# Three pairs of accumulator banks, coefficients by VectorE, ungated row gathers, and sparser breaks in the front's gathers

## The reference, cut to what matters

```python
z = jnp.einsum('ni,hoi->nho', h, Wfc)                       # 3750 x 8 x 64
e = jax.nn.leaky_relu(s_src[src] + s_dst[dst], negative_slope=NEG_SLOPE)
m = jax.ops.segment_max(e, dst, num_segments=N)
ex = jnp.exp(e - m[dst])
denom = jax.ops.segment_sum(ex, dst, num_segments=N)
alpha = ex / denom[dst]
msg = alpha[:, :, None] * z[src]
out = jax.ops.segment_sum(msg, dst, num_segments=N)
```

## Time and profile before

| | us |
|---|---|
| median of 3 runs | 4323.76 |
| lowest and highest run | 4310.84, 4329.1 |
| the profiled execution, device time | 4364.62 |
| its span, first to last instruction | 4362.9 |
| aggregation of layer 0, POOL's first gather to the end | 578.7 to about 1440 |
| aggregation of layer 1 | 2886.9 to about 3765 |

### The profile page before, as it was taken

How to read it: one execution, slowest core, us unless ns; L and a number is a source line. 1 busy time by engine, 2 the same in 40 slices (tenths; PEclk the granted TensorE clock), 3 DMA queues, 4 the chain that set the end, 5 groups by cost and what they waited for, 6 DMA issues and landing times. The chain is left out here.

```text
span 4362.9 us, 56022 instructions
## 1 busy us (share of the span) xinstructions
PE 3068.3 (70%) x12306; PEld 2004.9 (46%) x12307; DVE 2384.3 (55%) x4094; ACT 932.0 (21%) x2416; POOL 1617.7 (37%) x1595
## 2 busy tenths in 40 slices
PE   6957547777777784299995966637777777555990
PEld 2423235555555453255542433325555555454760
DVE  5756655555565786723324123565555555786444
ACT  2100012222222561011111200012222222341210
POOL 0565035555555000144431455135555555101215
PEclk9978768888898885599997987858888888757995
DMA  4315235555555112055555253124545555215336
GB/s 143 91 57 95 76 111 146 145 149 145 147 146 150 47 73 87 18 127 148 148 127 136 76 127 71 59 87 141 146 141 144 143 145 144 73 58 176 120 121 222
DMA packets 330652, 513.30 MB, mean 118 GB/s; under 512 B 172484, under 2 KB 177860, under 8 KB 329744
## 3 DMA queue, kind: packets, MB, share of 16 engines
q0 software_dynamic: 113824, 311.79, 26.8%
q1 hardware_dynamic: 92720, 194.54, 12.7%
q10 hardware_dynamic: 123840, 3.94, 1.6%
HBM read 423.20 MB, written 86.92 MB: 117 GB/s over the span
## 5 line engine op out<-in xcount | busy, mean ns | idle before, releaser
L898 POOL DMA_INDIRECT aggregate_zg<-z_rows,src_groups x940 | 890.6, 947 | 1061.0 <-SPq L906 480.6
L965 PE MATMUL bank<-aggregate_msg,aggregate_onehot 128*128 128x260 f32 x2816 | 818.5, 443 | 108.6 <-DVE aggregate_msg L932 77.7
L965 PEld LDWEIGHTS bank<-aggregate_msg,aggregate_onehot 128*128 128x128 f32 x2816 | 580.5, 217 | 215.7 <-issue 124.0
L932 DVE TENSOR_TENSOR aggregate_msg<-aggregate_zg,bank 128x1024 f32<-128x1024 f32 x528 | 639.8, 1212 | 11.2 <-SPq L911 5.3
L862 ACT COPY acc<-bank x530 | 313.9, 592 | 1221.0 <-PE bank L952 632.7
L927 DVE TENSOR_SCALAR aggregate_onehot<-bank,step_base,dst_groups 128x128 f32<-128x128 f32 x704 | 256.8, 406 | 503.3 <-PE bank L952 171.5
L369 POOL DMA_INDIRECT front_d<-src_scores,src_chunks x320 | 319.5, 998 | 347.2 <-DMA front_d<-src_scores,src_chunks 182.9
L952 PE MATMUL bank<-zero_bf 128*128 128x2 bf16 x1060 | 122.2, 171 | 301.3 <-ACT acc L862 217.0
L952 PEld LDWEIGHTS bank<-zero_bf 128*128 128x128 bf16 x1060 | 111.0, 105 | 438.8 <-issue 375.3
L965 PE MATMUL bank<-aggregate_msg,s_src 128*128 128x260 f32 x704 | 236.6, 466 | 59.2 <-DVE aggregate_msg L932 49.1
L1584 POOL DMA_INDIRECT exp_xg<-hn_rows,exp_gather_tok x64 | 71.9, 1124 | 537.0 <-DVE exp_gather_tok L1646 415.9
(11 more groups left out here) (378 smaller groups left out, 4204.7 us busy)
## 6 DMA issues: line engine op xcount, KB each, us to landing
exp_w<-in_L_ffn_w SPq DMA_DIRECT2D x32, 1024.0 KB
slot_out<-exp_y SPq DMA_DIRECT2D x66, 256.0 KB
z_rows<-front_z SPq DMA_DIRECT2D x60, 256.0 KB
hn_rows<-fin_xn SPq DMA_DIRECT2D x20, 768.0 KB, 3.4
aggregate_zg<-z_rows,src_groups POOLq DMA_INDIRECT x940
front_early<-src_key SPq DMA_DIRECT2D x16, 640.0 KB
front_early<-src_tile SPq DMA_DIRECT2D x16, 640.0 KB
front_edge<-src_key SPq DMA_DIRECT2D x16, 640.0 KB
```

The costliest lines, as they stand in the source:

```text
L898: pool.indirect_dma_start(zg[:, r, j, :], None, k.z_rows[:, :], bass.IndirectOffsetOnAxis(k.src_groups[:, n:n + 1], 0)).then_inc(gathered[ ...
L932: v.tensor_tensor(msg[:, m, :, 0:HD].rearrange("p u (h d) -> p u h d", d=DH), z, bcast_last(scale[n % COEF].rearrange("p (u h) -> p u h", ...
L965: nc.tensor.matmul(k.banks[:, bank(t, half), 0:HW].rearrange("p a n -> p (a n)"), lanes_of(n % OS, j), msg[:, m, j * 2 + half, :], start=F ...
```

## The change

In the aggregation there are three pairs of accumulator banks, used in turn. DVE builds, for each step, one packed register value in `step_tile`: the tile in the upper bits, and the first banks of the present, the next and the previous pair in three fields below. PE's opening of step n waits for `evict(n)`, where it waited for `evict(n+1)`. The lane numbers are read from SBUF (`k.iota`) and not from PSUM. The coefficients are copied to banks 6 and 7 by DVE, 16 groups at a time (15 copies in a layer), and ACT's copy to `scale` and its wait for `msg_ready` are gone; PE, and no longer DVE, waits for `prepared`. POOL's wait for the gather three before is gone. In the front, POOL waits after every eighth gather or scatter.

```diff
@@ front
-                            if c % 4 == 2:
+                            if c % 8 == 4:
                                 pool.wait_ge(gathered[i * J + j], 16 * c)
...
-                    if n % 4 == 2:
+                    if n % 8 == 4:
                         pool.wait_ge(scattered, 16 * n)
...
+                    tile, third, last = steps_i[0:1, 1, :], steps_i[0:1, 0, :], steps_f[0:1, :]
+                    packed = k.step_tile[:, LATE:]
+                    v.tensor_scalar(packed, tile, 512.0, 272.0, ALU.mult, ALU.add)
+                    chain(v.tensor_scalar(third, tile, 43.0, None, ALU.mult))
+                    chain(v.tensor_single_scalar(third, third, 7, ALU.logical_shift_right))
+                    chain(v.scalar_tensor_tensor(third, third, -3.0, tile, ALU.mult, ALU.add))
+                    v.tensor_scalar(last, third, 2.0, None, ALU.is_equal)
+                    chain(v.scalar_tensor_tensor(packed, third, -238.0, packed, ALU.mult, ALU.add))
+                    chain(v.scalar_tensor_tensor(packed, last, 336.0, packed, ALU.mult, ALU.add))
...
@@ aggregate
-        lanes = k.ps[4][:, 0:P]
-        scale = [k.ps[5 + u][:, 0:J * H] for u in range(COEF)]
+        lanes = k.iota[:, :]
+        scales = k.banks[:, 6:8, :].rearrange("p b n -> p (b n)")
+        scales_ready = sem("scales_ready")
...
                     act.wait_ge(evicted, n + 1)
-                    t = act.value_load(k.step_tile[0:1, bass.ds(n, 1)], min_val=0, max_val=NT - 1)
+                    x = act.value_load(k.step_tile[0:1, n:n + 1], min_val=0, max_val=(NT - 1) * 512 + 272)
                     act.wait_ge(summed, n + (HEAD - 1))
-                    nc.scalar.copy(k.acc_all[:, bass.ds(t * 2, 2), :], k.banks[:, bass.ds(((t + 1) & 1) * 2, 2), 0:HW]).then_inc(evicted, 1)
+                    nc.scalar.copy(k.acc_all[:, bass.ds((x >> 9) * 2, 2), :], k.banks[:, bass.ds((x >> 6) & 6, 2), 0:HW]).then_inc(evicted, 1)
...
-                    if n >= COEF:
-                        act.wait_ge(msg_ready, n)
...
-                    nc.scalar.copy(msg[:, n % MS, :, HD:HW], coef.rearrange("p (u h) -> p u h", u=J * 2))
-                    nc.scalar.copy(scale[n % COEF], coef).then_inc(prepared, 1)
+                    nc.scalar.copy(msg[:, n % MS, :, HD:HW], coef.rearrange("p (u h) -> p u h", u=J * 2)).then_inc(prepared, 1)
...
-                        if n >= IN_FLIGHT:
-                            f, i = divmod(n - IN_FLIGHT, J)
-                            pool.wait_ge(gathered[f % SLOTS][i], (f // SLOTS + 1) * 16)
...
-                v.memset(k.banks[:, 0:4, :], 0.0)
-                v.tensor_copy(lanes, k.iota[:, :]).then_inc(cleared, 1)
-                dve.wait_ge(cleared, 1)
+                v.memset(k.banks[:, 0:6, :], 0.0).then_inc(cleared, 1)
+                def load_scales(b):
+                    g, wide = b * SCALE_BLOCK, min(SCALE_BLOCK, NGR - b * SCALE_BLOCK) * J * H
+                    at = g % SCALE_RING * J * H
+                    return v.tensor_copy(scales[:, at:at + wide], k.alpha[:, g * J * H:g * J * H + wide]).then_inc(scales_ready, 1)
...
+                    if n % SCALE_BLOCK == 0 and n < NGR:
+                        dve.wait_ge(scales_ready, n // SCALE_BLOCK + 1)
+                    if n % SCALE_BLOCK == SCALE_BLOCK // 2 and n + SCALE_BLOCK // 2 < NGR:
+                        load_scales(n // SCALE_BLOCK + 1)
...
-                    dve.wait_ge(prepared, n + 1)
...
-                                    bcast_last(scale[n % COEF].rearrange("p (u h) -> p u h", u=J * 2), DH), ALU.mult).then_inc(msg_ready, 1)
+                                    bcast_last(scales[:, bass.ds((g & (SCALE_RING - 1)) * (J * H), J * H)].rearrange("p (u h) -> p u h", u=J * 2), DH), ALU.mult).then_inc(msg_ready, 1)
...
                     pe.wait_ge(msg_ready, n + 3)
+                    pe.wait_ge(prepared, n + 1)
...
-                    pe.wait_ge(evicted, n + 3)
-                    open_tile(t + 1).then_inc(summed, 1)
+                    pe.wait_ge(evicted, n + 2)
+                    open_tile((x >> 3) & 6).then_inc(summed, 1)
```

More of the change, by code:

```diff
@@ L51 @@
 OS = 3
-COEF = 3
+SCALE_BLOCK = 16
+SCALE_RING = 64
 SLOTS = 8
-IN_FLIGHT = 3
 LATE = 1
@@ L557, in _ @@
                     v.tensor_copy(steps_i[:, 1, :], ck)
-                    v.tensor_scalar(k.step_base[:, :], ck, float(P), None, ALU.mult)
+                    chain(v.tensor_scalar(k.step_base[:, :], ck, float(P), None, ALU.mult))
+                    tile, third, last = steps_i[0:1, 1, :], steps_i[0:1, 0, :], steps_f[0:1, :]
[7 more added lines that the diff above has]
+                    chain(v.scalar_tensor_tensor(packed, last, 336.0, packed, ALU.mult, ALU.add))
                     chain(v.tensor_tensor(steps_f, k.steps[:, :], ck, ALU.subtract))
                     chain(v.tensor_copy(steps_i[:, 0, :], steps_f))
-                    v.memset(k.step_tile[:, 0:LATE], 0)
+                    v.memset(k.step_tile[:, 0:LATE], 272)
                     v.memset(k.step_group[:, STEPS:], 0)
                     v.tensor_copy(k.group_freed[:, :], freed[0:1, 0:NGR])
-                    v.tensor_copy(k.step_group[:, 0:STEPS], steps_i[0:1, 0, :])
-                    chain(v.tensor_copy(k.step_tile[:, LATE:], steps_i[0:1, 1, :]))
+                    chain(v.tensor_copy(k.step_group[:, 0:STEPS], steps_i[0:1, 0, :]))
             @block.tensor
@@ L870, in prepare @@
                     coef = k.alpha[:, bass.ds(g * (J * H), J * H)]
-                    nc.scalar.copy(msg[:, n % MS, :, HD:HW], coef.rearrange("p (u h) -> p u h", u=J * 2))
-                    nc.scalar.copy(scale[n % COEF], coef).then_inc(prepared, 1)
+                    nc.scalar.copy(msg[:, n % MS, :, HD:HW], coef.rearrange("p (u h) -> p u h", u=J * 2)).then_inc(prepared, 1)
                 act.sem_inc(evicted, 1)
-                act.sem_inc(msg_ready, 2)
                 act.wait_ge(cleared, 1)
@@ L883, in _ @@
                 act.wait_ge(summed, STEPS + HEAD)
-                nc.scalar.copy(k.acc_all[:, NT * 2:, :], k.banks[:, (NT - 1) % 2 * 2:(NT - 1) % 2 * 2 + 2, 0:HW]).then_inc(evicted, 1)
+                nc.scalar.copy(k.acc_all[:, NT * 2:, :], k.banks[:, (NT - 1) % 3 * 2:(NT - 1) % 3 * 2 + 2, 0:HW]).then_inc(evicted, 1)
                 act.wait_ge(evicted, STEPS + 3)
@@ L917, in _ @@
                 v = nc.vector
-                v.memset(k.banks[:, 0:4, :], 0.0)
-                v.tensor_copy(lanes, k.iota[:, :]).then_inc(cleared, 1)
-                dve.wait_ge(cleared, 1)
+                v.memset(k.banks[:, 0:6, :], 0.0).then_inc(cleared, 1)
[3 more added lines that the diff above has]
+                    return v.tensor_copy(scales[:, at:at + wide], k.alpha[:, g * J * H:g * J * H + wide]).then_inc(scales_ready, 1)
+                dve.sem_inc(msg_ready, 2)
+                load_scales(0)
                 for n in range(STEPS):
                     m = n % MS
+                    if n % SCALE_BLOCK == 0 and n < NGR:
+                        dve.wait_ge(scales_ready, n // SCALE_BLOCK + 1)
+                    if n % SCALE_BLOCK == SCALE_BLOCK // 2 and n + SCALE_BLOCK // 2 < NGR:
+                        load_scales(n // SCALE_BLOCK + 1)
                     g = dve.value_load(k.step_group[0:1, n:n + 1], min_val=0, max_val=NGR - 1)
@@ L946, in _, with open_tile @@
             def _(pe):
-                bank = lambda t, half: bass.ds((t & 1) * 2 + half, 1)
-                def open_tile(t):
+                bank = lambda b, half: bass.ds(b + half, 1)
+                def open_tile(b):
                     for half in range(2):
-                        mm = nc.tensor.matmul(k.banks[:, bank(t, half), 510:512].rearrange("p a n -> p (a n)"), k.zero_bf[:, :], k.zero_bf[:, 0:2],
+                        mm = nc.tensor.matmul(k.banks[:, bank(b, half), 510:512].rearrange("p a n -> p (a n)"), k.zero_bf[:, :], k.zero_bf[:, 0:2],
                                               start=True, stop=True, skip_group_check=True)
@@ L960, in _ @@
                     m = n % MS
-                    t = pe.value_load(k.step_tile[0:1, n + LATE:n + LATE + 1], min_val=0, max_val=NT - 1)
+                    x = pe.value_load(k.step_tile[0:1, n + LATE:n + LATE + 1], min_val=0, max_val=(NT - 1) * 512 + 272)
                     pe.wait_ge(msg_ready, n + 3)
+                    pe.wait_ge(prepared, n + 1)
                     for j in range(J):
                         for half in range(2):
-                            nc.tensor.matmul(k.banks[:, bank(t, half), 0:HW].rearrange("p a n -> p (a n)"), lanes_of(n % OS, j), msg[:, m, j * 2 + half, :],
+                            nc.tensor.matmul(k.banks[:, bank(x & 6, half), 0:HW].rearrange("p a n -> p (a n)"), lanes_of(n % OS, j), msg[:, m, j * 2 + half, :],
                                              start=False, stop=True, skip_group_check=True)
-                    pe.wait_ge(evicted, n + 3)
-                    open_tile(t + 1).then_inc(summed, 1)
```

(2 more changed lines are left out.)

## The result

| | us |
|---|---|
| kernel before, median of 20 runs | 4322.15 (4303.81 to 4348.13) |
| changed kernel, median of 20 runs | 4296.03 (4252.65 to 4317.6) |
| ratio, with its 95% interval | 0.9921 (0.9897 to 0.9945) |
| profiled execution, before and after | 4364.62, 4264.45 |

The change makes the kernel 0.8% faster, 26 us by the medians and 34 us by the ratio, where 330 us were forecast, and the time lies above the range. The two profiled executions stand 100 us apart. That is too much: the one of before is above each of the 20 runs in the table, and the one of after is the third lowest of its own.

What follows compares the result with a forecast made beforehand. The prediction took PE's late opening signals, with PE held by its wait on the newest copy, as the bound. Its terms, -346 + 40 + 51 + 5 - 80 = -330 us, gave 3994 us; the range of 8 in 10 was 3840 to 4180 us.

Steps and rivals of the forecast that it cites:

- The wait moved by one step, -346 us: Aggregation: PE's later wait lets it work through late signals, gaining 3.17 us on each of 109, 346 us in all.
- The rival of the records that run ahead of the work: Aggregation: PE's matmuls really finish after the late signal, so its lead is unusable; 4129 us, chance 0.11.
- the second term against it: Aggregation: late signals may get longer, taken as 0.4 us on each of 128, 51 us; ends 0 and 640 us.
- The 19 more stalls (40 us): Aggregation: late signals come in proportion to POOL's work, 128 of them, 19 more, at 2.1 us each, 40 us.
- No limit, no gain, and a price of 51 us: Aggregation: dropping POOL's wait for the gather three before gains nothing, as POOL waits for slots instead; longer signals cost 51 us.
- Coefficients and lane numbers, nothing: Aggregation: coefficient copies and one-hots reading SBUF gain 0; extra copies, bank clearing and small front operations add 5 us at most.
- the rival of the blocked POOL: Aggregation: one-hots from SBUF block POOL's issue through the shared port, up to 143 us a layer; 4125 us, chance 0.08.
- The front, -80 us: Front: half as many breaks of picks and scatters save 36 us in layer 0 and 44 in layer 1, together 80.
- Nearly to POOL's floor: Aggregation: late signals wholly covered and PE's matmuls quicker, 640 us a layer; 3785 us in all, chance 0.14.
- Slower: Aggregation: without the limit each late signal lasts the 9 us of the filling, 977 us a layer; 4459 us, chance 0.07.
- The change does not reach the loop: Aggregation: another wait for the same opening holds PE, so only the front's 80 us come; 4244 us, chance 0.06.
- the two signs of being wrong: Aggregation: late signals of 7 us and more fill it, or PE still stops one step after a late opening.

Runs made afterwards that it cites:

- the limit of two: The changed kernel with POOL waiting for the gather two before (at most two under way and one being issued); 4531.6 us, ratio 1.0386 of the kernel before.

## Why the prediction was wrong

**What bounds the kernel.** Read rightly for the chip of the profile: PE's signals come late and everything stops behind them. What the prediction didn't see is that this isn't the kernel's own. On the four chips with before at some 4010 us no trace shows any of it, and then the aggregation is bound by POOL and the landing of gathers.

**The wait moved by one step, -346 us.** The lead is there: in the timeline PE opens twice and stops one step later. The rival of the records that run ahead of the work is out, by the two signals that come 0.13 us apart. The failed step is the second term against it, "I take 0.4 us on each, 51 us". The signals came 1.6 us later each ahead of the one-hots (5.5 against 3.9), 112 x 1.6 = 180 us. The length was taken as the signal's own, with only the removed limit to lengthen it, while it goes with POOL's: a late signal comes some 2 us after POOL has stopped, and POOL stops when the ring is full. The step that PE and DVE can now do in a stall frees one more group, so that POOL can issue two more gathers, 2.5 us, before it stops. Call the gathers between two pauses of over 1 us a burst: before, a burst had 4.6 gathers in the mean and the pause 2.6 us; now it is 7.4 and 4.1 us, and 97 of 127 bursts are of just eight. It is not the limit that kept them short: the kernel before without its limit still has bursts of 4.6. The pause by gather is 0.55 us in both, 516 us in all before and 513 us now, where the forecast of 745 us for a layer left room for some 150 us a layer: the stall has grown with the lead, and the stage has stayed. The 19 more stalls (40 us) didn't come either; there are three more by the count of rows 3, and eight fewer by that of the copies. The 180 us, which hold the limit's 38 us already, don't make up the whole gap between -346 and the 12 to 27 us that were measured; the rest isn't settled one by one.

**No limit, no gain, and a price of 51 us.** With late signals this part was about right: the limit alone costs 38 us, by stalls 0.4 to 0.5 us longer, where 0.4 us were taken. So what the term left out is not the limit's share but the lead's. Without late signals the part is wrong: the removed limit is two thirds of the whole gain. That its waits add to 49.3 us told little, since in that profile POOL waited 480.6 us for slots behind the stalls; where they are gone, POOL's waits of both kinds make 173 us a layer.

**Coefficients and lane numbers, nothing.** Right. A one-hot from SBUF takes 0.342 us (it was 0.405), not the 0.27 of the estimate; the issue of a gather stayed as it was, in the changed kernel's layer 0 (min/median/max ns):

```profile
L900 POOL DMA_INDIRECT aggregate_zg<-z_rows,src_groups x470: 941/946/1034, 549.9 to 1379.1; - x157
```

Thus the rival of the blocked POOL is out: one-hots from SBUF leave the issue at 0.95 us.

**The front, -80 us.** The breaks are half as many at 2.16 and 1.94 us. The two traces of before and after show 28.8 + 41.9 = 71 us, the runs of the front alone 45 to 60 us where signals are late, and some 100 us are left for it where they aren't. So the term of 80 us was right in its order, up to 35 us too large on the one kind of chip and some 20 us too small on the other; why it differs wasn't tried.

**The rivals.** "Nearly to POOL's floor", 3785 us, is what happens on a chip without late signals: 640 us a layer were forecast, 595 came, 3732 us in all. "Slower" had the right mechanism (without the limit a late signal lasts longer) at the wrong size: 9 us were taken, 5.7 came, under its point of decision of 7.3 us. (By the prediction's own terms the parts that are kept bring 346 - 40 - 5 + 80 = 381 us and not 415, which puts that point at 7.0 us. "POOL is blocked" would come to 4085 us and not 4125, since the 40.8 us between the profiled execution and the median were left out there.) "The change does not reach the loop" is out too: PE opens twice in a stall. Neither of the two signs of being wrong came: the late signals stayed under 7 us in the mean, and PE stopped a step later. It was the signs of being right that failed: PE's wait for the copy under 60 us (315.3 came), aggregations of 700 to 790 us (854), and POOL's wait for slots well below 480.6 us (518.8).

## What to carry to other kernels

A stall that ends when another engine stops is not shortened by giving its victims more lead: look at what the other engine does in the last microseconds before the stall ends, in every stall, before taking its length as a constant. A limit on transfers under way can be a cost on one chip and a gain on another; run both kernels on several chips when a trace has idle time that no record explains. Where such signals come late, the changed kernel with a break before every fourth gather took 0.958 of before, and without it 0.992 (two chips, so 3.4% is a comparison of ratios); where they don't, the break costs 10% (4099 against 3732 us on one chip).

## What the runs showed of the hardware

- On two of the six chips, and where the result was measured, PE's semaphore signals are seen late while POOL issues indirect gathers of 256 KB every 1.25 us: in bursts of two with 1.9 us between them (0 stalls), of four with 1.9 us (33 stalls of 2.2 us), of 4.6 (125 of 3.9 us), of 7.4 (117 of 5.7 us), and in the first filling, 22 in a burst, one signal 18.9 us late. On a chip of the other kind a burst of 470 held up none.
- It is PE's signals alone. Of the additions to semaphores that the trace of the changed kernel has in its aggregations, all 866 of ACT and all 400 of DVE come 0.01 us after the end of their instruction; 221 of PE's 511 come more than 1.5 us after its latest opening. On the third chip all 528 of PE come after 0.01 us.
- The gathers themselves aren't slower there: the first of a gather's 16 completions comes 2.8 to 3.0 us (median) after the issue begins on both kinds of chips. But the trace loses records: all 16 completions are recorded for 8 to 20% of the gathers in the kernels with bursts of four and more there, for 72% with the limit of two, and for 95 to 100% on the other chips. In the stall shown above the queues of PE, ACT and SP also do single register instructions in some 0.7 us that take 0.02 to 0.15 us otherwise. In both aggregations 306 of some 15,200 such instructions take over 0.45 us in the changed kernel, 83 of 14,100 in the kernel before, 12 with bursts of four, none with the limit of two, and none in any trace of the other four chips. What carries the signals and records, and why it differs between chips or times, is open.
- PE's granted clock is 0.84 to 0.90 in the aggregations of the kernels with 115 stalls and more, and 0.97 to 0.99 in those of 593 to 828 us, the one with 33 short stalls among them. It is 0.87 and 0.69 in those of 970 and 1353 us, which have no stall but where PE waits for gathers. So a low clock alone is no sign of late signals.
